# Expert scores of a fused attention and expert layer cross to the hidden units' rows by DMA through DRAM

## The chip, the cores and the metric

The kernel runs on one core of a Trainium2 chip. The metric is the device time of one execution in microseconds (us). Five engines work beside each other: TensorE (PE in the profile, its weight loads PEld), VectorE (DVE), ScalarE (ACT), GpSimd (POOL) and SyncE (SP), which only issues DMAs here.

## The reference, cut to what matters

64 batches of 128 tokens with 128 features each go through a cross attention over 120 context rows and then through a dense mixture of eight experts. Each token gets one score per expert, zero where the expert isn't among the token's first k (k is sampled by a small "actor" network):

```python
x = x + xattn(layernorm(x), ctx, ...)
h = layernorm(x)
probs = softmax(h @ router_w.T)                       # 8 experts
k = argmax(clip(gelu(h @ w1.T + b1) @ w2.T + b2)) + 1
scores = where(rank < k, probs, 0.0)
for e in range(8):                                    # 336 hidden units each
    y = (silu(h @ gate_w[e].T) * (h @ up_w[e].T)) @ down_w[e].T
    out = out + scores[..., e:e + 1] * y
x = x + out
```

All experts are computed for all tokens, and the score of an expert multiplies its hidden units.

## The kernel before, in words

The 64 batches are worked on in 16 **blocks** of four (BB = 4), so a block has 512 tokens (NT). The 8 x 336 hidden units are cut into 21 **tiles** of 128 rows: 16 units of each of the eight experts (ROWS = 16). Row r of a tile belongs to expert r // 16, whichever tile it is. So one array `score_bc` [128 rows, 512 tokens] per block, where the score of expert e stands in rows 16e to 16e+15, serves all 21 tiles of the block.

For each tile j: TensorE makes gate and up products (`gate`, `up`: three fp16 products of 128x512 each, L392 to L394, since every fp32 factor is split into a high and a low half), ScalarE takes the silu (L636), GpSimd multiplies it by `score_bc` (`weigh`, L819), VectorE multiplies by the up product (`hidden`, L1079), ScalarE takes the high half (`high`, L630), VectorE the low half (`low`, L1085), and TensorE adds the tile's down product (`down`, three more products).

Each engine's order is written out by hand: `turn(t, par)` runs slots j = 0 to 20 for block t. In slot j TensorE does the gate product of tile j+2, the up product of tile j and the down product of tile j-3; ScalarE does `high` of tile j-1 and the silu of tile j+2; GpSimd weighs tile j+1, so tile 0 of block t+1 is weighed in slot 20 of turn t; VectorE does `hidden` of tile j and `low` of tile j-1. Between them, in slots named by numbers, stands the work for later blocks: attention and second norm of block t+2, actor, router and ranks of block t+1, key products and first norm of block t+3. Turns 0 to 3 and 12 to 16 are written out, and turns 4 to 11 are a loop over pairs of turns. The rings are short: two gate banks, three up banks, three buffers of silu and of weighted; `high` and `hid_lo` have seven.

The scores of block t+1 are made by VectorE in slot 15 of turn t (`scores`, L1065: `score`, tokens on the rows, 4 x 8 values in each). They reach `score_bc` like this:

- slot 16, GpSimd, `split_scores` (L807, L808, L810): high and low fp16 halves into `score16`
- slot 17, TensorE, `score_transposes` (L331): four transposes into the bank x0; ScalarE, `score_copy` (L612): to `score_t`, fp16, 16 rows
- slot 19, TensorE, `score_broadcast` (L337): one product of 16 rows x 512 with a 0/1 matrix `sel_sb`, which sums the halves and spreads each expert over its 16 rows, into x0; ScalarE, `score_spread` (L617): to `score_bc[par]`

GpSimd then waits on `bc_ready` before it weighs tile 0. `turn_x` (L294), the next user of x0 for attention, waits on `bc_ready` too.

SyncE issues in turn t: the context of block t+4 (L254, waits for the value products of slot 10), x of block t+4 (L250, waits for `x2_ready`, slot 15 of VectorE), and the result of block t-1 (L278, waits for `out_ready`, slot 17 of VectorE). The first reader of that x is `stats_1` on VectorE (L916) in slot 0 of turn t+1.

Of the kernel before, what the change touches and what calls it, by code (L numbers as in the profile page):

```python
# [7 lines left out]
F32 = mybir.dt.float32  # L8
# [6 lines left out]
P = 128  # L15
BATCHES, CTX = 64, 120
BB = 4
NT = BB * P
NC = BB * CTX
BLOCKS = BATCHES // BB  # L20
EXPERTS, HIDDEN = 8, 336
# [46 lines left out]
def program(nc, x, ctx_t, consts, consts16, gate_t, up_t, down_t, out):  # L68
    x_blocks = x.rearrange("(t b p) d -> t p b d", b=BB, p=P)
    out_blocks = out.rearrange("(t b p) d -> t p b d", b=BB, p=P)  # L70
    ctx_blocks = ctx_t.rearrange("p (t n) -> t p n", n=NC)

    with ExitStack() as stack:
        def sb(name, shape, dt=F32):
# [2 lines left out]
        def sem(name):  # L77
            return stack.enter_context(nc.semaphore(name))
# [7 lines left out]
        def const(width, rows=P):  # L86
# [120 lines left out]
                             "over_ready", "score_ready"))  # L207
        s16hi_ready, s16_ready, st_done, st_ready, bc_done, bc_ready = (
            sem(n) for n in ("s16hi_ready", "s16_ready", "st_done", "st_ready", "bc_done", "bc_ready"))

        gate_done, up_done, silu_ready, weighted_ready, hid_ready, hid_hi_ready, hid_lo_ready, down_done = (
            sem(n) for n in ("gate_done", "up_done", "silu_ready", "weighted_ready", "hid_ready", "hid_hi_ready",
# [4 lines left out]
        def wait(eng, s, value):  # L217
            if not isinstance(value, int) or value > 0:
                eng.wait_ge(s, value)

        def is_block(n):
            return not isinstance(n, int) or 0 <= n < BLOCKS
# [4 lines left out]
        def upto(n):  # L227

            return min(n + 1, BLOCKS) if isinstance(n, int) else n + 1
# [16 lines left out]
        @block.sync  # L246
        def _(sp):
            def load_x(n, par):
                wait(sp, x2_ready, n - 1)
                sp.dma_start(x_in[par][:], x_blocks[n]).then_inc(x_loaded[par], 16)  # L250

            def load_ctx(n, par):
                wait(sp, vp_done, n - 1)
                sp.dma_start(ctx_in[par][:], ctx_blocks[n]).then_inc(ctx_loaded[par], 16)  # L254

            def load_weights(k, w):
                for c in range(3):
                    cols = slice(c * PART * P, (c + 1) * PART * P)
                    sp.dma_start(raw[k][:, cols], w[:, cols]).then_inc(weights_in[3 * k + c], 16)

            load_x(0, 0)
            load_ctx(0, 0)
            load_x(1, 1)
            load_ctx(1, 1)
            load_weights(0, gate_t)
            load_weights(1, up_t)
            load_weights(2, down_t)
            for n in range(2, 4):
                load_ctx(n, n % 2)
                load_x(n, n % 2)  # L270

            def turn(t, par):
                if is_block(t + 4):
                    load_ctx(t + 4, par)
                    load_x(t + 4, par)
                if is_block(t - 1):
                    sp.wait_ge(out_ready, t)
                    sp.dma_start(out_blocks[t - 1], out_sb[1 - par][:]).then_inc(stored[1 - par], 16)  # L278

            turns(sp, turn)  # L280
            for par in range(2):
                sp.wait_ge(stored[par], 16 * (BLOCKS // 2))

        @block.tensor
        def _(pe):
            mm, transpose = nc.tensor.matmul, nc.tensor.transpose

            def turn_x(n, dst=x0):
                pe.wait_ge(xn_ready, n + 1)
                if dst is x0:  # L290
                    wait(pe, x2_ready, n)
                    wait(pe, bc_ready, upto(n - 2))
                for b in range(BB):
                    last = transpose(dst[:, b * P:(b + 1) * P], xn_nat[:, b, :], ident_sb)  # L294
                last.then_inc(t1_done, 1)
# [150 lines left out]
            def turn(t, par):  # L446
                nxt = 1 - par
                for j in range(TILES):
                    if isinstance(t, int) and t == 0 and j == 2:
                        weights_turned(1, 2, 3)  # L450
                    if isinstance(t, int) and t == 0 and j == 4:
                        weights_spread(1, 2, 3)
                    if j == 1 and is_block(t + 1):
                        turn_x2(t + 1)
                    if j == 3 and is_block(t + 1):
                        actor_router(t + 1)
                    if j == 4 and is_block(t + 2):
                        turn_x(t + 2)
                    if j == 7 and is_block(t + 2):
                        energies(t + 2)  # L460
                    if j == 8 and is_block(t + 1):
                        logits(t + 1)
                    if j == 10 and is_block(t + 2):
                        values(t + 2, par)
                    if j == 12 and is_block(t + 2):
                        probs_transposes(t + 2)
                    if j == 14 and is_block(t + 2):
                        attend(t + 2)
                    if j == 15 and is_block(t - 1):
                        result_transposes(t - 1)  # L470
                    if j == 17 and is_block(t + 1):
                        score_transposes(t + 1)
                    if j == 18 and is_block(t + 3):
                        keys(t + 3, nxt)
                    if j == 19 and is_block(t + 1):
                        score_broadcast(t + 1)
                    if is_tile(TILES * t + j + LEAD):
                        if j + LEAD < TILES:
                            gate(t, par, j + LEAD)
                        else:  # L480
                            gate(t + 1, nxt, j + LEAD - TILES)
                    if is_tile(TILES * t + j):
                        up(t, par, j)
                    if isinstance(t, int) and t == 0:
                        for k in range(TILES):
                            if j == max(FIRST_DOWN + k // 2, k + LAG):
                                down(t, par, k)
                    elif is_tile(TILES * t + j - LAG):
                        if j >= LAG:
                            down(t, par, j - LAG)  # L490
                        else:
                            down(t - 1, nxt, j - LAG + TILES)
# [32 lines left out]
        def _(act):  # L525
# [113 lines left out]
            def turn(t, par):  # L639
                nxt = 1 - par  # L640
                for j in range(TILES):
# [33 lines left out]
                        norm1(t + 3, nxt, 0, 2)  # L675
                    if j == 14 and is_block(t + 3):
                        norm1(t + 3, nxt, 2, BB)
                    if j == 17 and is_block(t + 1):
                        score_copy(t + 1)
                    if j == 18 and is_block(t + 3):  # L680
                        keys(t + 3)
                    if j == 19 and is_block(t + 1):
                        score_spread(t + 1, nxt)
                    if j == 19 and is_block(t + 2):
                        norm2(t + 2, 0, 2)
                    if j == 20 and is_block(t + 2):
# [48 lines left out]
        def _(pool):  # L735
# [76 lines left out]

            def weigh(t, par, j):
                n = TILES * t + j
                if j == 0:
                    pool.wait_ge(bc_ready, t + 1)
                pool.wait_ge(silu_ready, n + 1)
                wait(pool, hid_ready, n - RING + 1)
                g.tensor_tensor(weighted[j % RING][:], silu[j % RING][:], score_bc[par][:], ALU.mult)\  # L819
                    .then_inc(weighted_ready, 1)  # L820

            def turn(t, par):
                nxt = 1 - par
                for j in range(TILES):
                    if is_tile(TILES * t + j + 1):
                        if j + 1 < TILES:
                            weigh(t, par, j + 1)
                        else:
                            weigh(t + 1, nxt, 0)
                    if j == 2 and is_block(t + 3):  # L830
                        rstd_1(t + 3)
                    if j == 3 and is_block(t + 1):
                        x2_low(t + 1, nxt)
                    if j == 11 and is_block(t + 1):
                        route_probs(t + 1)
                    if j == 11 and is_block(t + 1):
                        count_less(t + 1)
                    if j == 12 and is_block(t + 1):
                        count_places(t + 1)
                    if j == 14 and is_block(t + 1):  # L840
                        rank_over(t + 1)
                    if j == 16 and is_block(t + 1):
                        split_scores(t + 1)
                    if j == 17 and is_block(t + 2):
                        rstd_2(t + 2)

# [15 lines left out]
        def _(dve):  # L862
# [198 lines left out]

            def scores(n):
                dve.wait_ge(over_ready, n + 1)
                wait(dve, s16_ready, n)
                v.scalar_tensor_tensor(score[:], rank_less[:], 0.0, prob[:], ALU.is_le, ALU.mult)\  # L1065
                    .then_inc(score_ready, 1)

# [209 lines left out]
```

## Time and profile before

| | |
|---|---|
| median of 3 runs | 814.08 us (812.65 to 814.83) |
| the profiled execution | 812.56 us |
| its span, first to last instruction | 810.8 us |
| PE busy | 784.4 us, 97% |
| DVE, ACT, POOL busy | 77%, 74%, 65% |
| mean granted TensorE clock | 0.985 |
| HBM traffic | 12.73 MB read, 4.19 MB written |

Busy times of the engines overlap. A product of 128x512 reads 0.38 us in the profile but the next one starts 0.215 us after it, since products are pipelined; so what an instruction on PE costs is read from the starts of its neighbours. A turn takes 47.9 us (from one start of the score step on DVE to the next). The times in this text count from the start of the span.

### The profile page before, as it was taken

To read this page: it belongs to the slowest core of one execution; us is meant where nothing else is said; L and a number is where in the kernel's file an instruction comes from. 1 tells how busy PE (TensorE), PEld (TensorE's weight loads), DVE (VectorE), ACT (ScalarE), POOL (GpSimd) and SP (SyncE) were. 2 spreads that over 40 slices of the span, in tenths; PEclk is the share of its full clock that TensorE was granted. 3 is DMA by queue.
4 is the path that set the end of the run, shared out by engine and by line. 5 is a ranking of instruction groups with operands and counts; after the bars stand their busy time and mean duration, and the time that the engine had idled before them with its cause. 6 is when DMAs were issued, how large, how long until landed. Compare 5 with 4: busy or idle time off the path is not lost.

```text
span 810.8 us, 14159 instructions
## 1 busy us (share of the span) xinstructions
PE 784.4 (97%) x3923; PEld 394.7 (49%) x3923; DVE 627.4 (77%) x1351; ACT 596.3 (74%) x1047; POOL 530.0 (65%) x621
## 2 busy tenths in 40 slices
PE   7598999999999999999999999999999999999997
PEld 4344454454545545454554545455454544544443
DVE  4898778787787868778786877878688786867775
ACT  3587777877777787777777777777777778777664
POOL 2385667667576776757767575776757676676663
PEclk9689999999999999999999999999999999999999
DMA  7100001000000100000000000000000000000000
GB/s 290 39 1 13 14 6 35 1 17 23 14 27 2 38 2 13 28 13 26 0 25 15 12 26 12 26 2 25 13 12 27 1 14 1 1 14 1 13 1 27
DMA packets 20846, 17.60 MB, mean 22 GB/s; under 512 B 944, under 2 KB 19504, under 8 KB 20784
## 3 DMA queue, kind: packets, MB, share of 16 engines
q1 hardware_dynamic: 20496, 16.45, 6.4%
q10 hardware_dynamic: 288, 0.48, 0.2%
q8 instruction: 20, 0.33, 0.2%
q14 instruction: 42, 0.34, 0.1%
HBM read 12.73 MB, written 4.19 MB: 21 GB/s over the span
## 4 chain that ended last, share of the span: by engine, by line
PE 89%; DVE 4%; issue 3%; POOL 2%; ACT 1%; DMA 1%; DVEq 0%; POOLq 0%; ACTq 0%
PE bank L392 26%; PE bank L394 25%; PE bank L393 25%; PE bank L388 2%; PE bank L323 2%; PE bank L315 2%; PE bank L306 2%; PE bank L351 1%; POOL weighted L819 1%; PE bank L344 1%; DVE bank L1079 1%; PE bank L377 1%; DVE hid_lo L1085 1%; PE bank L294 1%; PE bank L362 1%
## 5 line engine op out<-in xcount | busy, mean ns | idle before, releaser
L819 POOL TENSOR_TENSOR weighted<-silu,score_bc 128x512 f32<-128x512 f32 x336 | 428.3, 1276 | 226.5 <-ACT silu L636 195.9
L1079 DVE SCALAR_TENSOR_TENSOR bank<-bank,h_scale,weighted 128x512 f32<-128x512 f32 x336 | 253.2, 754 | 141.0 <-PE bank L394 118.0
L630 ACT ACTIVATE hid_hi<-bank 128x512 f16<-128x512 f32 x336 | 200.4, 597 | 150.7 <-DVE bank L1079 146.0
L636 ACT ACTIVATE silu<-bank,silu_scale 128x512 f32<-128x512 f32 x336 | 230.9, 687 | 35.4 <-PE bank L394 34.2
L1085 DVE TENSOR_TENSOR hid_lo<-bank,hid_hi 128x512 f16<-128x512 f32 x336 | 228.2, 679 | 11.8 <-ACT hid_hi L630 11.7
L392 PE MATMUL bank<-xn_lo,gate_hi 128*128 128x512 f16 x336 | 128.5, 383 | 4.9 <-DVE gate_lo L909 4.9
L392 PE MATMUL bank<-xn_lo,up_hi 128*128 128x512 f16 x336 | 127.6, 380 | 0.8 <-DVE hid_lo L1085 0.7
L394 PE MATMUL bank<-xn_hi,gate_hi 128*128 128x512 f16 x336 | 128.1, 381 | 0.0
L393 PE MATMUL bank<-xn_hi,gate_lo 128*128 128x512 f16 x336 | 128.1, 381 | 0.0
L392 PE MATMUL bank<-hid_lo,down_hi 128*128 128x512 f16 x336 | 127.4, 379 | 0.6 <-DVE hid_lo L1085 0.6
L393 PE MATMUL bank<-xn_hi,up_lo 128*128 128x512 f16 x336 | 127.6, 380 | 0.0
L394 PE MATMUL bank<-xn_hi,up_hi 128*128 128x512 f16 x336 | 127.6, 380 | 0.0
L393 PE MATMUL bank<-hid_hi,down_lo 128*128 128x512 f16 x336 | 127.3, 379 | 0.0
L394 PE MATMUL bank<-hid_hi,down_hi 128*128 128x512 f16 x336 | 127.3, 379 | 0.0
L392 PEld LDWEIGHTS bank<-xn_lo,up_hi 128*128 128x128 f16 x336 | 32.9, 98 | 41.9 <-DVE hid_lo L1085 2.3
L392 PEld LDWEIGHTS bank<-xn_lo,gate_hi 128*128 128x128 f16 x336 | 34.3, 102 | 38.5 <-issue 15.1
L392 PEld LDWEIGHTS bank<-hid_lo,down_hi 128*128 128x128 f16 x336 | 32.9, 98 | 41.0 <-DVE hid_lo L1085 1.5
L394 PEld LDWEIGHTS bank<-xn_hi,gate_hi 128*128 128x128 f16 x336 | 33.0, 98 | 40.2 <-issue 0.8
L394 PEld LDWEIGHTS bank<-xn_hi,up_hi 128*128 128x128 f16 x336 | 32.9, 98 | 39.8 <-issue 0.3
L394 PEld LDWEIGHTS bank<-hid_hi,down_hi 128*128 128x128 f16 x336 | 32.9, 98 | 39.7
L393 PEld LDWEIGHTS bank<-xn_hi,up_lo 128*128 128x128 f16 x336 | 32.9, 98 | 39.4 <-issue 0.3
L393 PEld LDWEIGHTS bank<-hid_hi,down_lo 128*128 128x128 f16 x336 | 32.9, 98 | 39.3
(141 smaller groups left out, 839.4 us busy)
## 6 DMA issues: line engine op xcount, KB each, us to landing
x_in<-in_x SPq DMA_DIRECT2D x16, 256.0 KB, 2.6
out<-out_sb SPq DMA_DIRECT2D x16, 256.0 KB, 2.3
ctx_in<-in_ctx_t SPq DMA_DIRECT2D x16, 240.0 KB, 2.7
raw_gate<-in_gate_t SPq DMA_DIRECT2D x3, 448.0 KB, 6.4
raw_up<-in_up_t SPq DMA_DIRECT2D x3, 448.0 KB, 8.1
raw_down<-in_down_t SPq DMA_DIRECT2D x3, 448.0 KB, 9.9
consts_sb<-in_consts ACTq DMA_DIRECT2D x1, 403.0 KB, 3.7
consts_sb<-in_consts ACTq DMA_DIRECT2D x1, 64.0 KB, 4.2
```

What stands on the lines that cost most here:

```text
L306: last = mm(dst[:, b * CTX:(b + 1) * CTX], xn_t[:, b * P:(b + 1) * P], k_t[:, b * CTX:(b + 1) * CTX], start=True, stop=True)
L315: last = mm(dst[0:CTX, b * P:(b + 1) * P], ctx_in[par][:, b * CTX:(b + 1) * CTX], wv_t, start=True, stop=True)
L323: last = mm(dst[:, b * P:(b + 1) * P], probs_t[:, b * P:(b + 1) * P], v_sb[:, b * P:(b + 1) * P], start=True, stop=True)
L388: mm(dst[:, 0:NC], key_t[:], ctx_in[par][:], start=True, stop=True).then_inc(kp_done, 1)
L392: mm(dst, w_hi[w][:, cols], lo, start=start, stop=False)
L393: mm(dst, w_lo[w][:, cols], hi, start=False, stop=False)
L394: return mm(dst, w_hi[w][:, cols], hi, start=False, stop=stop)
L630: af(hid_hi[j % HRING][:], up_bank[j % U_BANKS][:], ACT.Copy).then_inc(hid_hi_ready, 1)
L636: af(silu[j % RING][:], gate_bank[(par + j) % G_BANKS][:], ACT.Silu, scale=silu_scale[:])\
L819: g.tensor_tensor(weighted[j % RING][:], silu[j % RING][:], score_bc[par][:], ALU.mult)\
L1079: v.scalar_tensor_tensor(up_bank[j % U_BANKS][:], up_bank[j % U_BANKS][:], h_scale[:], weighted[j % RING][:], ALU.mult, ALU.mult).then_inc ...
L1085: v.tensor_tensor(hid_lo[j % HRING][:], up_bank[j % U_BANKS][:], hid_hi[j % HRING][:], ALU.subtract)\
```

## The change

Block 0's scores go as before. From block 1 on, `split_scores`, `score_transposes`, `score_copy`, `score_broadcast` and `score_spread` are gone. In their place SyncE waits for `score_ready` and issues four DMAs (`send_scores`), one per batch of the block, from `score[:, b, :]` (128 rows x 8 values of 4 bytes) to a DRAM array `score_rows` [8, 4, 128], tokens innermost: each value goes to an address of its own. When all four have landed (`score_out`), a fifth DMA (`spread_scores`) reads each expert's row of 512 values for 16 rows of `score_bc` (256 KB to SBUF). GpSimd waits for that DMA (`score_in`) before tile 0. The scores step of VectorE waits until the sends of the block before have landed.

The load of x for block t+4 now stands between the sends and the spread in SyncE's order, and the result of block t-1 stands behind the spread.

```diff
+    score_rows = nc.dram_tensor("score_rows", (EXPERTS, BB, P), F32).ap()
...
+            def send_scores(n):
+                sp.wait_ge(score_ready, n + 1)
+                for b in range(BB):
+                    sp.dma_start(score_rows[:, b, :].rearrange("e p -> p e"), score[:, b, :],
+                                 allow_slow_non_contiguous=True).then_inc(score_out, 16)
+
+            def spread_scores(n, par):
+                sp.wait_ge(score_out, 16 * BB * n)
+                rows = score_rows.rearrange("e b p -> e (b p)").unsqueeze(1).broadcast_to([EXPERTS, ROWS, NT])
+                sp.dma_start(score_bc[par][:], rows).then_inc(score_in[par], 16)
+
             def turn(t, par):
                 if is_block(t + 4):
                     load_ctx(t + 4, par)
+                if is_block(t + 1):
+                    send_scores(t + 1)
+                if is_block(t + 4):
                     load_x(t + 4, par)
+                if is_block(t + 1):
+                    spread_scores(t + 1, 1 - par)
                 if is_block(t - 1):
                     sp.wait_ge(out_ready, t)
...
                 pe.wait_ge(xn_ready, n + 1)
                 if dst is x0:
                     wait(pe, x2_ready, n)
-                    wait(pe, bc_ready, upto(n - 2))
+                    if isinstance(n, int) and n == 2:
+                        pe.wait_ge(bc_ready, 1)
...
-                    if j == 17 and is_block(t + 1):
-                        score_transposes(t + 1)
...
-                    if j == 19 and is_block(t + 1):
-                        score_broadcast(t + 1)
...
-                    if j == 17 and is_block(t + 1):
-                        score_copy(t + 1)
...
-                    if j == 19 and is_block(t + 1):
-                        score_spread(t + 1, nxt)
...
             def weigh(t, par, j):
                 n = TILES * t + j
-                if j == 0:
-                    pool.wait_ge(bc_ready, t + 1)
+                if j == 0 and isinstance(t, int) and t == 0:
+                    pool.wait_ge(bc_ready, 1)
+                elif j == 0:
+                    pool.wait_ge(score_in[par], 8 * (t + par))
...
-                    if j == 16 and is_block(t + 1):
-                        split_scores(t + 1)
...
             def scores(n):
                 dve.wait_ge(over_ready, n + 1)
-                wait(dve, s16_ready, n)
+                if isinstance(n, int) and n == 1:
+                    dve.wait_ge(s16_ready, 1)
+                else:
+                    wait(dve, score_out, 16 * BB * (n - 1))
```

On TensorE, slots 16 to 20 of a turn before (L331 are the four transposes, L337 the spreading product, L388 the key product of slot 18):

```order
L331 MATMUL bank<-consts_sb,score 16x128 [waits x2_ready,s16_ready]
L331 MATMUL bank<-consts_sb,score 16x128 x3
L392 MATMUL bank<-xn_lo,gate_hi 128x512 [waits silu_ready]
...
L388 MATMUL bank<-ctx_in,key_t 128x480 [waits ptt_ready,al_ready,out_ready,ctx_loaded0]
L392 MATMUL bank<-xn_lo,gate_hi 128x512 [waits silu_ready]
...
L394 MATMUL bank<-hid_hi,down_hi 128x512
L337 MATMUL bank<-score_t,consts_sb 128x512 [waits st_ready]
L392 MATMUL bank<-xn_lo,gate_hi 128x512 [waits silu_ready,lo_ready,hi_ready]
```

The same place now (lines are 21 higher; L409 is the key product):

```order
L413 MATMUL bank<-hid_lo,down_hi 128x512 [waits hid_lo_ready]
L414 MATMUL bank<-hid_hi,down_lo 128x512
L415 MATMUL bank<-hid_hi,down_hi 128x512
L409 MATMUL bank<-ctx_in,key_t 128x480 [waits ptt_ready,al_ready,out_ready,ctx_loaded0]
L413 MATMUL bank<-xn_lo,gate_hi 128x512 [waits silu_ready]
```

The five products and their waits are gone, and nothing takes their place. On SyncE, one turn of the loop before:

```order
L254 ISA [waits vp_done]
L254 DMA ctx_in<-in_ctx_t 128x480
L250 ISA [waits x2_ready]
L250 DMA x_in<-in_x 128x4x128
L278 ISA [waits out_ready]
L278 DMA out<-out_sb 128x4x128
```

And now:

```order
L256 ISA [waits vp_done]
L256 DMA ctx_in<-in_ctx_t 128x480
L277 REGISTER_ALU
L279 DMA score_rows<-score 128x8x1 [waits score_ready]
L279 DMA score_rows<-score 128x8x1 x3
L252 ISA [waits x2_ready]
L252 DMA x_in<-in_x 128x4x128
L283 ISA
L285 DMA score_bc<-score_rows 128x1x512 [waits score_out]
L298 ISA [waits out_ready]
L298 DMA out<-out_sb 128x4x128
```

Five DMAs per turn are added, and the load of x and the store of the result stand behind some of them.

## Rows read from the trace of the kernel before

**Rows 1.** The page: engine busy times, and busy tenths in 40 slices
```profile
PE 784.4 (97%) x3923; PEld 394.7 (49%) x3923; DVE 627.4 (77%) x1351; ACT 596.3 (74%) x1047; POOL 530.0 (65%) x621
...
PE   7598999999999999999999999999999999999997
```

**Rows 2.** Stretches of one turn: busy us (instructions) per engine, clock, DMA share, GB/s
```profile
329.00:377.00 48.00, 48.00 (x246) 24.35 (x245) 37.73 (x82) 36.75 (x66) 32.66 (x39) 1.00 0.06 17
```

**Rows 3.** PE's instructions at slots 17 and 19 of turn 6 (start us, us)
```profile
374.65 0.38 PE L394 MATMUL bank<-hid_hi,down_hi 128*128 128x512 f16 x1
374.96 0.39 PE L331 MATMUL bank<-consts_sb,score 128*16 128x128 f16 x4
375.28 0.39 PE L392 MATMUL bank<-xn_lo,gate_hi 128*128 128x512 f16 x1
375.50 0.38 PE L393 MATMUL bank<-xn_hi,gate_lo 128*128 128x512 f16 x1
...
379.76 0.38 PE L394 MATMUL bank<-hid_hi,down_hi 128*128 128x512 f16 x1
380.07 0.39 PE L337 MATMUL bank<-score_t,consts_sb 16*128 16x512 f16 x1
380.39 0.39 PE L392 MATMUL bank<-xn_lo,gate_hi 128*128 128x512 f16 x1
```

**Rows 4.** The score step and its readers on DVE and ACT in turn 6
```profile
371.79 0.47 DVE L1065 SCALAR_TENSOR_TENSOR score<-rank_less,prob 128x32 f32<-128x32 f32 x1
...
381.91 0.59 ACT L617 ACTIVATE score_bc<-bank 128x512 f32<-128x512 f32 x1
```

**Rows 5.** The page, DMA issues: count, KB each, median us from issue to landing
```profile
x_in<-in_x SPq DMA_DIRECT2D x16, 256.0 KB, 2.6
out<-out_sb SPq DMA_DIRECT2D x16, 256.0 KB, 2.3
```

**Rows 6.** SyncE's issues in turn 6
```profile
372.94 0.37 SPq L250 DMA_DIRECT2D x_in<-in_x  x1
377.09 0.40 SPq L278 DMA_DIRECT2D out<-out_sb  x1
```

**Rows 7.** Short stretches around those two DMAs; the last two columns are DMA share and GB/s
```profile
372.94:373.94 1.00, 1.00 (x6) 0.47 (x5) 1.00 (x2) 0.46 (x1) 1.00 (x1) 1.00 0.00 0
373.94:375.10 1.16, 1.16 (x9) 0.44 (x7) 1.16 (x6) 0.71 (x2) 1.08 (x5) 1.00 0.75 225
375.10:375.60 0.50, 0.50 (x6) 0.27 (x5) 0.50 (x2) 0.10 (x1) 0.50 (x1) 1.00 0.01 2
...
378.00:379.10 1.10, 1.10 (x6) 0.48 (x5) 0.20 (x1) 0.46 (x2) 1.10 (x2) 1.00 0.77 238
```

**Rows 8.** The stretch of one context load, 128 pieces of 1,920 bytes
```profile
359.85:362.60 2.75, 2.75 (x15) 1.25 (x13) 1.12 (x3) 2.71 (x6) 0.12 (x1) 1.00 0.30 89
```

**Rows 9.** From weighing tile 0 of block 7 to the products behind it
```profile
382.74 1.27 POOL L819 TENSOR_TENSOR weighted<-silu,score_bc 128x512 f32<-128x512 f32 x1 [1.83 <-DVE bank L1079]
383.91 0.76 DVE L1079 SCALAR_TENSOR_TENSOR bank<-bank,h_scale,weighted 128x512 f32<-128x512 f32 x1 [0.59 <-PE bank L394]
...
384.98 0.60 ACT L630 ACTIVATE hid_hi<-bank 128x512 f16<-128x512 f32 x1
385.18 0.86 DVE L916 BATCH_NORM_STATS2 stats<-x_in 128x6 f32<-128x128 f32 x4
...
385.46 0.70 ACT L636 ACTIVATE silu<-bank,silu_scale 128x512 f32<-128x512 f32 x1
...
388.10 0.59 ACT L567 ACTIVATE xn_t<-bank 128x512 f32<-128x512 f32 x1
...
390.64 0.65 PE L351 MATMUL bank<-xn_t,consts_sb 128*64 128x256 f32 x4
...
391.49 1.27 POOL L819 TENSOR_TENSOR weighted<-silu,score_bc 128x512 f32<-128x512 f32 x1
```

**Rows 10.** DVE's instructions in slots 15 to 17 of turn 6
```profile
373.36 0.67 DVE L1085 TENSOR_TENSOR hid_lo<-bank,hid_hi 128x512 f16<-128x512 f32 x1
```

More of the change, by code:

```diff
@@ L209, in program @@
             sem(n) for n in ("s16hi_ready", "s16_ready", "st_done", "st_ready", "bc_done", "bc_ready"))
+        score_out, score_in = sem("score_out"), [sem(f"score_in{k}") for k in range(2)]
         gate_done, up_done, silu_ready, weighted_ready, hid_ready, hid_hi_ready, hid_lo_ready, down_done = (
```

## The prediction

> **What bounds the kernel now.** I read the page first: PE is busy 97% of the span and stands at 9 tenths in every slice but the first two, the fifth and the last [rows 1]. Then a turn as one stretch: from 329 to 377 us PE is busy 48.00 of 48.00 us at the full granted clock, while DVE, ACT and POOL have 10 to 15 us to spare [rows 2]. So in the steady turns TensorE is the bound, and its own instructions set the pace: what is taken off PE there comes off the time, as long as every operand is still there in time. Last I read the instructions in order of time around the scores, to see what the five removed products cost on PE, when the scores are made and when they are first needed.
>
> **What is removed.** A 128x512 product starts 0.215 us after the one before it. At slot 17 the product ahead of the four transposes starts at 374.65 and the one behind them at 375.28, 0.63 us later: the transposes cost 0.63 - 0.215 = 0.415 us. At slot 19 the pair around the spreading product stands at 379.76 and 380.39: again 0.415 us [rows 3]. That is 0.83 us per turn, and 15 turns (blocks 1 to 15): **12.4 us off PE**. All of it lies on the path, for PE has no gap to lose it in. Could DVE stop PE from taking it? At slot 17 PE needs the low half of tile 14 for the up product of tile 17 (its up bank), some 0.65 us behind the first gate product at 375.28; that half was done by 374.03 [rows 3, 10]. It leaves almost 2 us, against 0.83 gained. On GpSimd three small steps and on ACT two copies (one of them the 0.59 us of [rows 4]) go as well. They are costed at nothing: both engines have idle time, PE's work covers it.
>
> **What is added: a chain of transfers.** The score step ends at 371.79 + 0.47 = 372.26, and today `score_bc` is ready at 381.91 + 0.59 = 382.50, 10.2 us later [rows 4]. The new chain has to be told from DMAs of other shapes.
>
> - SyncE wakes and issues; an issue takes 0.37 to 0.40 us, whatever its size here [rows 6]. The first data moves 1.0 us after an issue (no DMA share in the first us after 372.94), and a load has landed within about 0.2 us of its last data [rows 7]. 0.1 + 1.0 us to the first send's data; the other three issues (3 x 0.4 us) run beside it.
> - The sends are 4 x 128 x 8 = 4,096 pieces of 4 bytes, 256 for each of the 16 engines. No row shows such a piece. The load of x has 512 pieces of 512 bytes and 16 completions; it used 0.75 of 16 engines for 1.16 us, so 1.16 x 0.75 x 16 / 528 = 26.4 ns each; the store to DRAM 1.10 x 0.77 x 16 / 528 = 25.7 ns [rows 7]. Pieces of 1,920 bytes cost 2.75 x 0.30 x 16 / 144 = 92 ns [rows 8], so most of a piece's time here is its bytes, and the straight line through 512 and 1,920 bytes leaves some 3 ns for an empty piece. Low end 3 ns. The high end is open, since no row shows what a write of 4 bytes to DRAM costs; I bound it by twice the nearest row, 53 ns, for an engine that had to read what is there and write it back. I take **26 ns**, the row of the smallest pieces: a price per piece is what such a list of pieces is likeliest to pay. 256 x 26.4 = 6.8 us (0.8 us, and then the four issues set it, to 13.6 us).
> - Landing 0.2, SyncE's wake 0.1, then the spread: 256 KB as the load of x, 2.6 us [rows 5]. The load of x that now stands ahead of it in the rings takes 1.1 us of data and fits into the spread's own 1.0 us start.
>
> Sum: 0.1 + 1.0 + 6.8 + 0.2 + 0.1 + 2.6 = **10.8 us**, between 5 and 17.6. The Trainium skill (DMA: Bandwidth & Descriptors, "Why a DMA increments its semaphore by 16 and not by 1") says that a DMA is split over the largest number of engines, up to 16, that divides the slowest dimension of both sides; the spread's source has 8 experts there, so it would run on 8 engines, and an estimate from the row of x doubles its 1.1 us of data, 11.9 us in all. No row of this trace shows a source of that shape, and the forecast is the same by either.
>
> **How late may the scores be?** In the trace PE reaches the first work that hangs on tile 0 of the new block at slot 3 (390.64, the actor and router products), 0.83 us sooner after the change, 389.8. They need ACT's copy of slot 1 (0.59 us, L567), which stands behind `high` of tile 0 (0.5) and the silu of tile 3 (0.6); `hidden` of tile 0 (0.76) and the weighing (1.27) stand before these [rows 9]. Back from 389.8 with about 0.2 us for hand-overs: weighing has to start at 385.9. That is 385.9 - 372.26 = **13.6 us** for the chain. At 10.8 us the chain fits with 2.8 us over. GpSimd starts tile 0 at about 383.1 instead of 382.74 and has caught up by the tile it weighs at 391.49, since it takes 1.27 us of a slot of 1.95 or more. In cost per piece the limit is (13.6 - 4.0) / 256 = 37 ns.
>
> **What else stands behind the sends.** The load of x was issued at 372.94 [rows 6]; it is now issued at about 374.1 and its data starts when the sends' is through, at 380.2: landed at 381.5. `stats_1` reads it at 385.18 [rows 9], 384.4 after the change: 2.9 us to spare. The result's store comes 6 us later than at 377.09, and its buffer is next written two turns on: no cost. The score step's new wait is for sends of the turn before: long over. `turn_x` loses a wait that was met early.
>
> **The sum.** The profiled execution took 812.56 us, 1.5 us below the median of the runs. 812.56 - 12.4 = 800.1; against the median, 814.08 - 12.4 = **801.6 us**, 1.5% faster. By its own uncertainties (the spread of the runs, a few tenths per turn at the edges) this case reaches from 799 to 804.
>
> **Rivals.**
> 1. *A write of 4 bytes costs a read and a write (slower).* At 53 ns per piece the sends take 13.6 us and the chain 17.6; the weighing of tile 0 starts 4.0 us past the limit in each of 15 turns. GpSimd's wait on the spread takes the place of the removed products: ACT stands behind `hid_hi` of tile 0, PE behind ACT. 15 x 4.0 = 60, less 12.4: 862 us. It decides from 37 ns (no gain lost) over 41 ns (nothing gained) up. For it: pieces of 4 bytes are far from every row here. Against it: in the rows a piece's time goes by its bytes. The Trainium skill (same page, "Specifications") states that an engine does a read-modify-write below 512 bytes; no row here shows a data piece under 512 bytes. 18%.
> 2. *Far slower (slower).* 4,096 writes to 16 KB of DRAM could also queue up behind each other at the memory, at 60 ns per engine or much more: from 890 us. Nothing in the trace speaks for or against it. 8%.
> 3. *Between the two.* 37 to 53 ns per piece, or the same delay from slower starts: some or all of the gain is given back, 802 to 860 us. 15%: 2 still faster, 5 within 0.3%, 8 slower.
> 4. *Hidden, but no gain.* PE sheds its products and then waits for DVE or GpSimd at another slot. Time unchanged, 814. Against it are the 10 us per turn that both have idle [rows 2] and the 2 us of [rows 10]. 2%.
> 5. *As forecast*, 57%.
>
> **The numbers.** 0.3% (2.4 us) is about what a measurement of this kernel can tell from no change. Faster 57 + 2 = 59%, same 5 + 2 = 7%, slower 8 + 18 + 8 = 34%. The predicted time is that of the likeliest case. The range has to take in most of rival 1, so it goes from 799 to 865 us; outside are rival 2, the upper part of rival 1, and a little below, 17% together. The forecast's own range is 799 to 804.
>
> **What would show each step.** PE: the turn shortens from 47.9 to 47.1 us, and PE stays busy without a gap, full clock. The landing of the four sends, issue to landing, should read 3 to 8 us, the spread's 2.6 to 3.3; from the end of the score step to the spread's landing 10.8 us. If POOL waits for the spread by more than 3 us beyond its other waits in each turn, and PE's first product of slot 3 or the actor and router products wait for ACT, rival 1 holds, and the share of DMA during the sends tells the cost of a piece. If DVE waits for x, the load behind the sends is the trouble. The prediction is wrong if a piece costs more than 37 ns.

## The result, and the profile after

The changed kernel takes **1057.5 us** (median of 4 runs, 1056.0 to 1059.4) against 813.4 for the kernel before: ratio 1.300 (95% interval 1.297 to 1.304). The forecast was 801.6 us with a range up to 865. It is 244 us slower, far outside.

The page of the changed kernel (engines; slices of 26 us: PE, granted clock, DMA share; one queue; DMA issues), to be held against [rows 1, 5]:

```profile
PE 814.4 (77%) x3848; PEld 397.2 (38%) x3848; DVE 627.0 (59%) x1351; ACT 581.3 (55%) x1017; POOL 517.4 (49%) x576
...
PE   5788694977949598694985949769596794949778
...
PEclk9699797998979889797997979979699896978979
DMA  6009056090730909128091370905608080180500
...
q1 hardware_dynamic: 84936, 20.64, 41.0%
...
x_in<-in_x SPq DMA_DIRECT2D x16, 256.0 KB, 21.9
out<-out_sb SPq DMA_DIRECT2D x16, 256.0 KB, 4.2
```

PE fell from 97% to 77%, with a hole in every turn, and in the holes the clock goes down and the DMA share up. The queue of SyncE moved 20.6 MB in 84,936 pieces, 61,440 of them the 4-byte values. The load of x, 2.6 us before, lands after 21.9.

The waits, summed (who waited, for whom; us in total, times, longest):

```profile
ACT hid_hi L647 <- DVE bank L1095: 376.0, 200, 19.0
POOL weighted L834 <- DMA score_bc<-score_rows: 299.2, 15, 21.0
...
PE bank L413 <- DVE hid_lo L1101: 206.1, 19, 16.1
...
DVE stats L929 <- DMA x_in<-in_x: 138.0, 13, 13.8
```

GpSimd waits for the spread in each of the 15 turns, 20 us on average; DVE waits for x in 13.

One turn (start us, us), first the score step, then SyncE, GpSimd and PE:

```profile
469.97 0.48 DVE L1081 SCALAR_TENSOR_TENSOR score<-rank_less,prob 128x32 f32<-128x32 f32 x1
...
470.48 2.24 SPq L279 DMA_DIRECT2D score_rows<-score  x4
472.91 1.75 SPq L252 DMA_DIRECT2D x_in<-in_x  x1
495.13 0.61 SPq L285 DMA_DIRECT2D score_bc<-score_rows  x1
...
499.31 4.94 POOL L834 TENSOR_TENSOR weighted<-silu,score_bc 128x512 f32<-128x512 f32 x4 [20.33 <-DMA score_bc<-score_rows]
...
502.01 0.61 PE L413 MATMUL bank<-xn_lo,up_hi 128*128 128x512 f16 x1 [13.96 <-DVE hid_lo L1101]
502.42 0.63 PE L414 MATMUL bank<-xn_hi,up_lo 128*128 128x512 f16 x1
```

The scores are ready at 470.45 (469.97 + 0.48). The sends are issued at once, but the spread only at 495.13, **24.7 us** after the first send (21.0 to 24.9 in the 15 turns), and tile 0 is weighed at 499.31: the chain takes 28.9 us where 10.8 were forecast. PE stands still for 14 us and comes back with products 0.42 us apart instead of 0.215.

Stretches of the same turn (busy us per engine as in [rows 2]; clock, DMA share, GB/s):

```profile
471.50:473.00 1.50, 1.50 (x8) 0.69 (x7) 1.50 (x7) 1.18 (x2) 0.81 (x2) 1.00 0.92 6
...
490.00:502.00 12.00, 0.00 (x0) 0.00 (x0) 2.26 (x7) 0.52 (x2) 2.69 (x3) 0.50 0.20 47
...
502.01:507.00 4.99, 4.99 (x14) 1.47 (x15) 2.83 (x8) 3.89 (x8) 4.91 (x8) 0.50 0.00 0
507.00:518.60 11.60, 11.60 (x63) 6.45 (x62) 8.17 (x14) 8.04 (x14) 7.45 (x7) 1.00 0.00 0
```

In the stretch in which PE is idle the granted clock is 0.50 (1.2 of 2.4 GHz), and the first 5 us of work run at it, which costs about 2.5 us (products 0.42 us apart instead of 0.215). The turn's account: 28.9 - 13.6 (what the kernel can bear, by the prediction) = 15.3 us late, plus 2.5 of slow clock, less 0.8 gained = 17.0. The measured turn is 64.6 us (ten turns, from the sends issued at 149.00 to those at 794.54, rows below) against 47.9, so 16.7; times 15 it makes 250, measured 244.

```profile
149.00 2.24 SPq L279 DMA_DIRECT2D score_rows<-score  x4
...
794.54 2.25 SPq L279 DMA_DIRECT2D score_rows<-score  x4
```

### The profile page after: what moved, and what is told of

The parts are those of the page before. It is cut to its first block, busy times and chain, and to the rows that moved or that the text cites. A ratio compares the mean times of both kernels' runs of the same rounds, so it can differ in the third digit from the quotient of the medians.

```text
span 1057.2 us, 13950 instructions
## 1 busy us (share of the span) xinstructions
PE 814.4 (77%) x3848; PEld 397.2 (38%) x3848; DVE 627.0 (59%) x1351; ACT 581.3 (55%) x1017; POOL 517.4 (49%) x576
## 3 DMA queue, kind: packets, MB, share of 16 engines
q1 hardware_dynamic: 84936, 20.64, 41.0%
## 4 chain that ended last, share of the span: by engine, by line
PE 44%; DMA 21%; issue 19%; DVE 8%; POOL 4%; ACT 2%; SPq 1%; DVEq 0%; POOLq 0%; ACTq 0%
DMA score_rows<-score 17%; PE bank L413 13%; PE bank L414 12%; PE bank L415 12%; POOL weighted L834 3%; DMA score_bc<-score_rows 3%; DVE hid_lo L1101 3%; DVE bank L1095 1%; PE bank L372 1%; SPq L279 1%; PE bank L336 1%; PE bank L327 1%; PE bank L409 1%; PE bank L344 1%; ACT silu L653 1%
## 5 line engine op out<-in xcount | busy, mean ns | idle before, releaser
L413 PE MATMUL bank<-xn_lo,up_hi 128*128 128x512 f16 x336 | 133.1, 396 | 205.6 <-DVE hid_lo L1101 205.5
L413 PE MATMUL bank<-xn_lo,gate_hi 128*128 128x512 f16 x336 | 131.6, 392 | 10.7 <-DVE gate_lo L922 5.1
L414 PE MATMUL bank<-xn_hi,up_lo 128*128 128x512 f16 x336 | 132.7, 395 | 0.0
L415 PE MATMUL bank<-xn_hi,up_hi 128*128 128x512 f16 x336 | 131.8, 392 | 0.0
L413 PE MATMUL bank<-hid_lo,down_hi 128*128 128x512 f16 x336 | 131.3, 391 | 0.6 <-DVE hid_lo L1101 0.6
L414 PE MATMUL bank<-xn_hi,gate_lo 128*128 128x512 f16 x336 | 131.6, 392 | 0.0
L414 PE MATMUL bank<-hid_hi,down_lo 128*128 128x512 f16 x336 | 131.2, 390 | 0.0
L415 PE MATMUL bank<-hid_hi,down_hi 128*128 128x512 f16 x336 | 131.2, 390 | 0.0
L415 PE MATMUL bank<-xn_hi,gate_hi 128*128 128x512 f16 x336 | 131.1, 390 | 0.0
L929 DVE BATCH_NORM_STATS2 stats<-x_in 128x6 f32<-128x128 f32 x64 | 13.9, 280 | 138.0 <-DMA x_in<-in_x 138.0
## 6 DMA issues: line engine op xcount, KB each, us to landing
x_in<-in_x SPq DMA_DIRECT2D x16, 256.0 KB, 21.9
```

Of the source, the lines that this page charges most:

```text
L413: mm(dst, w_hi[w][:, cols], lo, start=start, stop=False)
L414: mm(dst, w_lo[w][:, cols], hi, start=False, stop=False)
L415: return mm(dst, w_hi[w][:, cols], hi, start=False, stop=stop)
L929: last = v.bn_stats(stats1[:, b, :], x_in[par][:, b, :])
```

## The experiments

**Is it the number of pieces, DRAM, or where they land?** Four kernels, each with the sends edited. The spread keeps its place and its 256 KB, but in the first it spreads the scores in another order, and from the second on it reads rows of x, so these kernels time the transfers and leave the scores out. A time without a ratio is that of one execution; the executions of the kernel before, in all these sessions, lay between 812.1 and 816.3 us. "First send to spread" is the time between the two issues in a turn near the middle (sends issued at 454 to 491 us). Whole tokens:

```diff
-    score_rows = nc.dram_tensor("score_rows", (EXPERTS, BB, P), F32).ap()
+    score_rows = nc.dram_tensor("score_rows", (BB, P, EXPERTS), F32).ap()
-        sp.dma_start(score_rows[:, b, :].rearrange("e p -> p e"), score[:, b, :], ...)
+        sp.dma_start(score_rows[b], score[:, b, :])
```

> The four sends write the 8 values of a token as one piece of 32 bytes, 128 pieces per send, tokens outermost in DRAM; the spread then reads the same 16 KB as 8 rows, so the rows hold the scores in another order (that part of the computation, the turning, is left out). Theory A (the sends are slow because each of 4,096 single 4-byte values is a write of its own to DRAM): issue of the first send to the spread's issue falls from 24.7 us to under 5 us, the spread lands within 9 us of the score step, PE stays busy, and the time is 800 to 804 us. Rival B (the slow part is the round trip through DRAM and its dependence, whatever the pieces): the chain stays over 15 us and the time over 900 us.

Measured: 803.3 us (before, beside it: 813.2). The spread is issued 2.9 us after the first send (2.8 to 2.9 in all turns but the last, 4.1). The round trip through DRAM is innocent (rival B falls).

To SBUF: the destination is `score_apart[:, b, :, 0]`, an SBUF array [128, 4, 8, 2].

> The same 4,096 values of 4 bytes as single pieces, but to an SBUF array (every second 4-byte place), nothing to DRAM; the spread reads rows of x. Theory A (DRAM writes are the price): a piece costs what the completions of 4 bytes showed, under 20 ns per engine, so the sends take under 7 us and the time is 800 to 804 us. Rival C (making or moving single pieces is the price, whatever the destination): 80 ns or more per piece, sends over 20 us, time near 1057 us.

Measured: 803.3 us, first send to spread 4.5 us. So 4,096 single pieces as such are cheap. The page counts as many pieces as in the changed kernel, at 11.9% of the engines' time instead of 41.0%:

```profile
q1 hardware_dynamic: 84936, 20.64, 11.9%
```

64 bytes for each value: `(EXPERTS, BB, P, 16)`, written at `[:, b, :, 0]`.

> The same 4,096 values of 4 bytes, but each goes to 64 bytes of its own in DRAM (the array is 16 times larger and only every 16th value is written); the spread reads rows of x instead, which leaves the scores out. Theory A1 (any write of 4 bytes to DRAM costs this much, wherever it lands): the sends still take 20 us or more and the time stays within 5% of 1057 us. Rival A2 (the writes queue up because 16 tokens of several engines fall into the same 64 bytes): the sends fall under 10 us and the time to 800 to 815 us.

Measured: 804.4 us, first send to spread 7.5 us. The same 4-byte writes to DRAM, each in 64 bytes of its own, are hidden but for 1 us. A1 falls, A2 stands.

A quarter: only `b == 0` is sent.

> Only the first of the four sends (1,024 values instead of 4,096); the spread reads rows of x. If the price is one per piece (24 us for 4,096), the send takes some 6 to 8 us, the spread has landed 11 to 12 us after the score step, within the 13.6 us that the kernel can bear, and the time is 800 to 806 us. If it is a wait that does not depend on the number of pieces, the time stays over 1000 us.

Measured: 920.3 us, first send to spread 16.2 us (13.3 to 16.2 in the 15 turns): both expectations missed. A quarter of the values takes some 0.6 of the time of all, so the price isn't one per piece. Nor are the DMA engines at work all this time. In the last three turns no x is loaded, so only the sends are under way. The single send of such a turn, and the four of the changed kernel's, with the stretches between first send and spread (columns as before):

```profile
745.57 0.36 SPq L279 DMA_DIRECT2D score_rows<-score  x1
759.87 0.65 SPq L285 DMA_DIRECT2D score_bc<-in_x  x1
...
745.57:747.30 1.73, 1.73 (x10) 0.79 (x9) 1.73 (x4) 0.91 (x2) 1.21 (x1) 1.00 0.27 2
747.30:759.80 12.50, 12.50 (x59) 5.81 (x58) 8.28 (x20) 8.19 (x16) 5.33 (x8) 1.00 0.00 0
```

```profile
856.95 2.24 SPq L279 DMA_DIRECT2D score_rows<-score  x4
881.57 0.61 SPq L285 DMA_DIRECT2D score_bc<-score_rows  x1
...
856.95:873.00 16.05, 16.05 (x76) 7.41 (x75) 10.00 (x23) 9.67 (x18) 6.55 (x8) 1.00 1.36 1
873.00:881.50 8.50, 0.59 (x3) 0.10 (x1) 0.00 (x0) 0.00 (x0) 0.00 (x0) 0.66 0.00 0
```

The engines are through with the 1,024 pieces after 1.7 us, and with the 4,096 after 16; then no packet moves for 12.5 and 8.5 us, and only then are the sends reported as landed. So a large part of the wait lies behind the engines' own work, and as the sends to SBUF have none of it, on the writes' way to DRAM. At what place there, no run shows. (A share over 1 means that packets of one engine overlap in the trace.)

**How near is too near?** The spacing was varied further, `(EXPERTS, BB, P, 4)` and `(..., 8)`, then the values of one token side by side at 8 bytes, `(BB, P, EXPERTS, 2)`, and at last packed as in the changed kernel but with rows 9 KB apart, `(EXPERTS, BB, 18 * P)`.

> Token order as in the changed kernel, but 16 bytes from one value to the next in DRAM: four values share 64 bytes instead of 16; the spread reads rows of x, the scores are left out. If the time of the sends goes by the number of values in one 64-byte stretch (24.6 us for 16, 7.5 us for 1), four give 10 to 12 us, just within what the kernel can bear: 802 to 825 us. If it goes by the number of different stretches or banks in another way (conflict or none), it is either that of 16 (over 1000 us) or that of 1 (804 us).

> As the runs with 16, 4 and 1 values in 64 bytes of DRAM (first send to spread 24.7, 15.0 and 7.5 us), now two: 32 bytes from one value to the next; the spread reads rows of x, the scores are left out. If the stretch in which single values hinder each other is 64 bytes, two give some 10 us from first send to spread and a time of 803 to 815 us; if it is 32 bytes or less, two are as free as one: 7.5 us and 804 us.

> 4,096 single values, now token-major in DRAM with 8 bytes from one to the next: eight values of one token share 64 bytes, and the same engine writes all eight one behind the other; the spread reads rows of x, the scores are left out. If only values from different engines hinder each other in one 64-byte stretch, the sends take under 6 us and the time is 800 to 806 us. If any two single writes to the same stretch queue up, and the time goes by how many fall into one stretch (8 here, 16 in the changed kernel with some 24 us), the sends take 8 to 14 us and the time is 802 to 850 us.

> 4,096 single values in the changed kernel's token order, side by side as there (16 in 64 bytes), but each of the 32 rows of 128 tokens starts 9 KB behind the one before, so the array covers 288 KB of DRAM, more than the 256 KB of the run with 64 bytes per value; the spread reads rows of x, the scores are left out. If values that share a short stretch (64 bytes) hinder each other, first send to spread stays at 20 us or more and the time over 1000 us. If what counts is over how much DRAM the writes are strewn (16 KB in the changed kernel), it falls to 7 or 8 us and the time to some 804 us.

| values in 64 bytes | first send to spread, us | in the 15 turns | time, us |
|---|---|---|---|
| 1 | 7.5 | 6.7 to 7.7 | 804.4 |
| 2 | 8.8 | 8.0 to 9.1 | 805.4 |
| 4 | 15.0 | 12.9 to 16.0 | 911.0 |
| 8, one token's | 21.5 | 19.2 to 22.2 | 1015.7 |
| 16 (the change) | 24.7 | 21.0 to 24.9 | 1057.5 |
| 16, rows 9 KB apart | 31.1 | 26.0 to 31.5 | 1121.3 |

Strewing the rows over 288 KB helps nothing, on the contrary: what counts is how many single values fall close together within a row of 128. Eight values of one token, all of one row of `score`, are hardly better than 16 of many tokens, though each token's row leaves SBUF as a run of neighbouring pieces: 21.5 us and 1015.7 us are over both of that run's expectations. The time of four missed its expectation too (10 to 12 us, 802 to 825), so it isn't in proportion to the number. The time falls with every step of the spacing, and 64 bytes was the widest that was tried, so the length of the stretch within which values hinder each other stays open; two in 64 bytes still cost 1.3 us over one.

**Is the late x a cause of its own?** Edit: SyncE issues `load_x` ahead of `send_scores`.

> The changed kernel with one move: SyncE issues the load of x ahead of the four sends instead of behind them. In the changed kernel VectorE idles 138 us in 13 places until x has landed. If that wait decides (the load queues behind the sends), x lands in 3 us again and the time falls by 100 us or more. If only the chain of sends and spread decides, the wait for x goes from the profile but the same idle time is then put down to GpSimd's weighing, the sends start some 0.7 us later, and the time is 1055 to 1075 us.

Measured: 1011.2 us, between both expectations (before, beside it: 814.7). x lands in 3.7 us, DVE's wait for it is gone, and the idle time is put down to GpSimd's weighing:

```profile
POOL weighted L834 <- DMA score_bc<-score_rows: 255.6, 15, 21.9
DVE bank L1095 <- POOL weighted L834: 209.9, 17, 19.9
```

So DVE's wait for x lay beside the chain. What was saved, 46 us, came from the chain: in 11 of the 12 turns that load x, first send to spread is now 16.7 to 21.2 us (24.6 in the other) instead of 22.7 to 24.9. It would be natural to say that x, queued behind the sends, had held them up. The last three turns speak against it: they load no x, and they take 24.6, 24.6 and 21.0 us in the changed kernel, as long as with x behind the sends, and 24.6, 25.6 and 22.7 in this one. With a load just ahead of them the sends are through sooner; why, no run shows.

**Do the sends hurt anyone but those who wait for them?** The kernel before, whole, plus the sends at the end of SyncE's turn, read by nobody; only the next turn's score step waits until they have landed.

> The kernel before, whole, with the changed kernel's four sends (4,096 values, turning, to DRAM) added at the end of each of SyncE's turns; nothing reads what they write and only the score step of the next turn waits for them. If they cost the changed kernel its time through the wait for them alone, this one takes the time before, 812 to 817 us. If moving them disturbs the other transfers or engines (the context of the next block, the result's store), it is over 825 us.

Measured: 889.8 us (883 to 900); ratio 1.091 (1.087 to 1.095) without the slowest of the four, the profiled one. It is the second case of the expectation, far above its 825 us, though nobody waits for the data within 40 us. Its waits, two moments on ACT, and the page's line for one of the two queues that load the engines' instructions, before and here:

```profile
ACT hid_hi L638 <- issue: 48.7, 4, 16.4
PEld bank L400 <- ACT silu L644: 44.1, 6, 14.5
...
466.89 0.88 ACT L561 ACTIVATE xn_nat<-x_all,shift,rstd 128x128 f32 x2
483.35 0.60 ACT L638 ACTIVATE hid_hi<-bank 128x512 f16<-128x512 f32 x1 [15.59 <-issue]
...
q14 instruction: 42, 0.34, 0.1%
q14 instruction: 43, 0.35, 0.4%
```

ACT stands still for 15.6 us with no operand missing that the profile shows, from 7.4 us after the sends of that turn were issued (460.38), and PE after it. Three such stops, in three of the 15 turns, make 48 of the 87 us by which this execution is longer; the rest is smaller stops. The packets of q14, about as many as before, take four times the share of the same 16 engines: one of 8 KB took at most 0.7 us before, and in each of the three stops there is one of 1.6 to 9.1 us. So instruction loads are slowed by the sends. That they are what ACT waited for fits "issue" and the moments, but wasn't isolated.

**A version without single values.** VectorE turns the scores in 32x32 squares:

```diff
+                v.scalar_tensor_tensor(score_eb[:].rearrange("p e b -> p b e"), rank_less[:], 0.0, prob[:],
+                                       ALU.is_le, ALU.mult).then_inc(score_ready, 1)
+                dve.wait_ge(score_ready, n + 1)
+                v.transpose(score_turned[:], score_eb[:].rearrange("p e b -> p (e b)")).then_inc(turned_ready, 1)
...
+                for q in range(BB):
+                    part = slice(q * 32, (q + 1) * 32)
+                    sp.dma_start(score_rows.rearrange("e b p -> (e b) p")[:, part], score_turned[part, :])
```

> From block 1 on VectorE turns the scores itself: the score step writes them expert-major (32 values per token), one transpose of 32x32 squares follows, and the four sends write 32 rows of 32 tokens each, 128 pieces of 128 bytes instead of 4,096 of 4; the rest is as in the changed kernel, all values are computed. Theory A2 (many single values that fall into one 64-byte stretch of DRAM queue up there): no value is written alone, the sends land in 2 us, the spread 7 us after the score step, and the full 12.4 us off TensorE remain: 800 to 804 us. Rival (the extra step on VectorE or the five DMAs hold something else up): over 806 us.

Measured: 806.8 us against 814.7, ratio 0.990 (0.988 to 0.991). The spread is issued 2.8 us after the first send, yet the gain is 7.9 us, not 12.4. SyncE, DVE and PE of one turn:

```profile
465.84 0.21 DVE L1092 STREAM_TRANSPOSE score_turned<-score_eb 128x32 f32<-128x32 f32 x1
...
466.08 1.73 SPq L282 DMA_DIRECT2D score_rows<-score_turned  x4
468.83 0.61 SPq L288 DMA_DIRECT2D score_bc<-score_rows  x1
...
470.12 0.66 DVE L1098 TENSOR_TENSOR out_sb<-bank,x_all 128x512 f32<-128x512 f32 x1
...
470.89 1.04 PE L412 MATMUL bank<-ctx_in,key_t 128*128 128x480 f32 x2 [0.40 <-issue]
```

The key product of slot 18 needs the bank that DVE's result addition of slot 17 reads (`out_ready`). The addition ends at 470.78, the product starts at 470.89, after 0.40 us of idle. In the kernel before, the addition ended at 472.71, and the product followed its neighbour at 473.02 without a gap:

```profile
472.06 0.65 DVE L1072 TENSOR_TENSOR out_sb<-bank,x_all 128x512 f32<-128x512 f32 x1
...
472.81 0.38 PE L394 MATMUL bank<-hid_hi,down_hi 128*128 128x512 f16 x1
473.02 0.97 PE L388 MATMUL bank<-ctx_in,key_t 128*128 128x480 f32 x2
```

Two ways to part them:

```diff
-                    if j == 18 and is_block(t + 3):    # keys, TensorE and ScalarE
+                    if j == 19 and is_block(t + 3):
```

> The version that turns the scores on VectorE (806.8 us), with the key products of block t+3 one slot later (slot 19 instead of 18, on TensorE and ScalarE). In that version TensorE waited 0.4 us per turn at slot 18, for VectorE's result addition that frees the bank. If that wait is why 7.9 us were gained instead of 12.4, it goes, and the time is 801 to 803.5 us; if the gain is limited elsewhere, the time stays at 806 us or more.

```diff
-                    if j == 17 and is_block(t - 1):    # result, VectorE
+                    if j == 16 and is_block(t - 1):
```

> The version that turns the scores on VectorE, with VectorE's result addition one slot earlier (slot 16 instead of 17), key products in their old slot 18. By the same theory the bank is free before the key products and the time is 801 to 804 us; but the hidden and low steps of slot 16 come 0.6 us later, and if TensorE then waits for these, it stays at 805 to 808 us.

Measured: **801.3 us**, ratio 0.985 (0.983 to 0.987), and **800.5 us**, ratio 0.984 (0.982 to 0.986), against 813.3. They gain 12.0 and 12.8 us, the whole 12.4 within the spread of the runs, and are faster than both kernels.

**Half the products.** Turn on TensorE in fp32, copy on ScalarE, spread by one DMA from SBUF:

```diff
-                    last = transpose(x0[0:2 * EXPERTS, :].bitcast(F16)[:, b * P:(b + 1) * P], score16[:, b, :], ...)
+                    last = transpose(x0[0:EXPERTS, b * P:(b + 1) * P], score[:, b, :], ident_sb)
...
+                sp.dma_start(score_bc[par][:], score_t32[:].unsqueeze(1).broadcast_to([EXPERTS, ROWS, NT]))
```

> The kernel before with one product of the two: the scores are turned on TensorE in fp32 (four transposes, no split into halves), ScalarE copies 8 rows to SBUF, and one DMA from SBUF to SBUF spreads them to the units' rows; no DRAM. The spreading product (0.415 us per turn) is gone, the transposes stay: half of the gain, 814 - 16 x 0.415 = 807 us (805 to 809) if the transfer is hidden. If a transfer whose source is 8 rows of SBUF is slow, the weighing waits for it and the time is over 812 us.

Measured: 808.7 us, ratio 0.993 (0.992 to 0.994): 6.0 us, half the gain, as expected. But this one transfer holds GpSimd up by 4 us in each turn, since it takes 7.6 us from issue to the weighing:

```profile
424.30 0.64 SPq L265 DMA_DIRECT2D score_bc<-score_t  x1
...
431.85 1.27 POOL L823 TENSOR_TENSOR weighted<-silu,score_bc 128x512 f32<-128x512 f32 x1 [3.96 <-DMA score_bc<-score_t]
```

Since 6.0 of the 6.6 us (16 x 0.415) were gained, that delay costs next to nothing: it comes within the slack.

## Why the prediction was wrong, step by step

- **The step that failed** is the price of a piece of 4 bytes: "a price per piece is what such a list of pieces is likeliest to pay", 26 ns, bounded by 53. The sends took 24.7 us, which by the prediction's own sum (1.0 us before, 0.2 behind) is some 23.5 us / 256 = 92 ns per piece and engine. The bound was the mistake: it was argued from a read and a write of one piece, and nothing in the rows limited how long neighbours hold each other up. For values apart the sum came out: with 64 bytes each, first send to spread took 7.5 us, where 1.0 + 6.8 + 0.2 = 8.0 were forecast. That is partly luck, since to SBUF the same number took 4.5 us and the 26 ns were borrowed from pieces of 512 bytes. No price per piece and engine describes the packed ones: in the turns without x the engines had no packet for the last 8.5 of 24.6 us, and a quarter of the values still took 13 to 16 us. The time goes by how densely single values lie in DRAM.
- Rival 2, writes that queue up behind each other at the memory ("from 890 us", 8%), is the one that the runs bear out, as far as they show that the wait lies behind the engines and goes by nearness in DRAM. It was given 8% because nothing in the trace spoke for or against it, and the range was cut below it; where no row bounds a cost, the range shouldn't be cut by the bound one chose. The Trainium skill (DMA: Bandwidth & Descriptors, "Specifications") has a read-modify-write below 512 bytes. Pieces of 4 bytes with 64 bytes of their own were hidden here, and pieces of 32 bytes took 2.9 us for all four sends: the density decides, the size alone doesn't. Whether a read-modify-write has a part in it, no run here shows.
- *The limit of 13.6 us* is borne out as far as it was tried. With 8.8 us from first send to spread, and some 4.2 more to the weighing as in the changed kernel, 13 us were hidden but for some 2 us (805.4 against 803.3 with the chain of 2.9); with 15.0, so 19, they were not (911 us). Nothing between was run. GpSimd waits, DVE behind it, then ACT and PE, as rival 1 told it. With 28.9 us the chain is 15.3 past the limit, some 230 us over 15 turns.
- *The load of x* was to have 2.9 us to spare. It landed after 21.9 us, and DVE waited for it in 13 turns, but beside the chain: with x first that wait was gone and GpSimd's took its place. That x first also saved 46 us was in no part of the prediction, and stays unexplained.
- *The spread*, 2.6 us by the row of x, takes 4.2 from issue to weighing, some 24 us over 15 turns. The trace holds 9 semaphore updates for each spread and 16 for a load of x, which fits the eight engines of the prediction's other sum; the number of engines was not varied.
- *The clock* wasn't in the sum: idle for 14 us, PE comes back at 0.50. That is about 2.5 us per turn, some 37 of the 244.
- *12.4 us off PE* was right as what TensorE sheds (two versions gained 12.0 and 12.8), but not all of it comes by itself. With the chain hidden and nothing else altered the gain was 10.0 us (803.3 against 813.2): the prediction checked tile 14's low half against slot 17 and passed over the key product's wait for `out_ready` at slot 18. In that run the key product of one turn starts 0.44 us after its neighbour (467.50, 467.94), behind the addition's end at 467.83, where it was 0.21 us before.
- That idle sends slow others was in no rival.
- *A small misreading:* the slice of rows 1 that stands below 9 is the fourth, not the fifth; nothing hangs on it.

## What to carry to other kernels

Turn data before it goes to DRAM, so that every piece is a run: the same 16 KB took 24.7 us as 4,096 packed single values and 2.8 us as 128-byte runs after one 0.21 us step on VectorE. When an instruction is taken off the bounding engine, check every wait of that engine in the slots behind it, for one that was met just in time can become the next stall. Where no row shows anything like a new operation, the honest range is wide, and a run that times the operation alone comes before a kernel that depends on it.

## What the runs showed of the hardware that wasn't expected

- Single 4-byte writes to DRAM hinder each other by nearness: 7.5, 8.8, 15.0, 21.5 and 24.7 us from first send to spread for 4,096 of them with 1, 2, 4, 8 and 16 in 64 bytes, and 13.3 to 16.2 us for a quarter of them with 16. In turns without another transfer the DMA engines are done with the packets 8.5 and 12.5 us before the sends count as landed.
- Such a jam reaches others: a load of 256 KB queued behind it landed after 21.9 us instead of 2.6, and in the run with idle sends ScalarE stopped three times for some 16 us with no wait that the profile shows, while instruction packets of 8 KB took up to 9.1 us instead of 0.7.
- A DMA that spreads 8 rows of SBUF over 128 took 7.6 us to the weighing, the one from DRAM 4.2.
